# Transposed h of tiles 5 to 7 and half of one x by DMA instead of TensorE pieces, four context loads issued later, in a gated two-layer block

## The reference

```python
q1 = fake_quant(layernorm(x), x1_scale, x1_zp)      # (2, 1024, 2048)
q2 = fake_quant(ctx, x2_scale, x2_zp)               # (2, 2048, 2048)
x  = x + tanh(g_xattn[0]) * (q1 @ q2)
x  = x + tanh(g_ffn[0]) * einsum('bti,oi->bto', layernorm(x), U * S[None, :] @ V.T)
```

## Time and profile before

| | |
|---|---|
| median of 3 runs | 603.96 us (603.78 to 606.05) |
| profiled execution, its own time | 604.71 us |
| its span on the core | 602.9 us |
| granted TensorE clock | 1.0 |
| PE busy | 582.7 us, 97% |
| DVE, ACT, POOL busy | 381.7, 212.4, 191.4 us |
| DMA moved | 102.21 MB |

### The profile page before, as it was taken

One profiled execution on the slowest core, in us unless ns is written; L12 is line 12 of the kernel. 1 busy time (PEld: TensorE's weight loads), 2 busy tenths in 40 slices (PEclk: granted clock), 3 DMA queues, 4 the chain that ended last, 5 costly groups with the idle time before them and its releaser, 6 DMA issues.

```text
span 602.9 us, 7571 instructions
## 1 busy us (share of the span) xinstructions
PE 582.7 (97%) x2816; PEld 266.4 (44%) x2816; DVE 381.7 (63%) x703; ACT 212.4 (35%) x258; POOL 191.4 (32%) x149
## 2 busy tenths in 40 slices
PE   1899999999999999999999999999999999999998
PEld 1344444444444444445444444444444444444444
DVE  6939989995288962845375975647365665735212
ACT  5798978822041432456623310303011030301000
POOL 2899650002223419726505800220404030030000
DMA  8999985639828795998835344370906345181512
GB/s 280 387 387 387 309 240 128 116 122 196 239 55 240 186 216 189 241 304 268 241 123 150 81 84 54 66 190 12 223 35 147 116 90 172 30 163 20 138 53 104
DMA packets 143828, 102.21 MB, mean 170 GB/s; under 512 B 106672, under 2 KB 106928, under 8 KB 143792
## 3 DMA queue, kind: packets, MB, share of 16 engines
q1 hardware_dynamic: 134800, 84.43, 53.1%
q10 hardware_dynamic: 8992, 17.30, 9.2%
HBM read 58.99 MB, written 16.78 MB: 126 GB/s over the span
## 4 chain that ended last, share of the span: by engine, by line
PE 75%; DMA 11%; DVE 8%; issue 3%; SPq 2%; ACT 1%; POOL 1%; DVEq 0%; ACTq 0%
PE bank L553 23%; PE bank L584 16%; PE bank L651 8%; PE bank L650 8%; PE bank L655 8%; PE bank L589 8%; DMA v_hl<-in_ctx_dram 8%; DMA xT<-xs 4%; DVE v_hl L1246 1%; DVE xn L1174 1%; DVE xs L1177 1%; DVE ring L1137 1%; SPq L311 1%; PE bank L520 1%; POOL u8r L243 1%
## 5 line engine op out<-in xcount | busy, mean ns | idle before, releaser
L553 PE MATMUL bank<-q,qT 128*128 128x512 bf16 x896 | 201.5, 380 | 0.3 <-DVE ring L1137 0.3
L553 PEld LDWEIGHTS bank<-q,qT 128*128 128x128 bf16 x896 | 87.7, 98 | 107.1 <-issue 1.5
L258 POOL TENSOR_SCALAR ring<-ring,bvec 128x2048 f32<-128x2048 f32 x16 | 32.8, 2050 | 269.7 <-DVE bvec L1119 269.7
L584 PE MATMUL bank<-v_hl,xT 128*128 128x512 f16 x512 | 115.8, 379 | 0.9 <-DMA xT<-xs 0.9
L263 POOL TENSOR_TENSOR ring<-ring,corr 128x512 f32<-128x512 f32 x64 | 87.0, 1390 | 23.2 <-ACT corr L850 22.1
L651 PE MATMUL bank<-u_hl,hbuf 128*128 128x512 f16 x240 | 91.1, 380 | 0.0
L650 PE MATMUL bank<-u_hl,hbuf 128*128 128x512 f16 x240 | 91.0, 379 | 0.0
L1137 DVE SCALAR_TENSOR_TENSOR ring<-bank,const,ring 128x512 f32<-128x512 f32 x64 | 47.6, 743 | 58.2 <-PE bank L553 55.9
L1210 DVE SCALAR_TENSOR_TENSOR ring<-bank,cy,ring 128x512 f32<-128x512 f32 x63 | 46.4, 747 | 52.8 <-PE bank L655 52.8
L252 POOL TENSOR_SCALAR q<-u8r,const 128x1024 bf16<-128x1024 uint8 x52 | 63.9, 1236 | 45.4 <-ACT u8r L756 41.7
L584 PEld LDWEIGHTS bank<-v_hl,xT 128*128 128x128 f16 x512 | 49.8, 98 | 61.2 <-DMA xT<-xs 1.9
(11 more groups left out here) (136 smaller groups left out, 493.3 us busy)
## 6 DMA issues: line engine op xcount, KB each, us to landing
out_dram<-ring SPq DMA_DIRECT2D x63, 256.0 KB, 3.5
ring<-in_x_dram SPq DMA_DIRECT2D x62, 256.0 KB, 3.9
v_hl<-in_ctx_dram SPq DMA_DIRECT2D x26, 512.0 KB, 11.5
stage<-in_ctx_dram ACTq DMA_DIRECT2D x17, 512.0 KB, 5.8
u_hl<-in_L_ffn_V_dram SPq DMA_DIRECT2D x8, 512.0 KB, 11.5
corr<-in_ctx_dram ACTq DMA_DIRECT2D x8, 512.0 KB, 6.7
stage<-in_ctx_dram SPq DMA_DIRECT2D x6, 512.0 KB, 11.5
q<-in_ctx_dram ACTq DMA_DIRECT2D x4, 512.0 KB, 8.8
```

The lines of the kernel that those rows point to most:

```text
L553: mm = nc.tensor.matmul(unit_bank(t, n)[:, :], qT_of(t)[:, k, :], q2[:, n, k, :], start=(k == 0), stop=(k == KT - 1))
L584: nc.tensor.matmul(h_bank(u)[:, :], xT[:, g, half, k % 8, :], v_hl[:, k, 0, :], start=(g == 0 and a == 0 and half == 0), stop=False)
```

## The change

Transposed h of tiles 5, 6 and 7 comes by DMA from SP, and so does half g = 0 of tile 7's x. Half g = 1 stays on PE. h of tile 5 is put into `qT`'s half 1 and h of tile 7 into half 0, so two waits are new: the DMA for h of tiles 5 and 7 waits until `s1` of tile 6 or 7 is over, and `q_transpose` of tiles 8 and 9 waits until `mm4` of tile 5 or 7 has read that half. h of tile 6 stays in `hT`, and its DMA waits for `mm4(4)`. ACT issues the four `room` loads behind `x_hi_half(7, 0)` and `stream(14, 17)` instead of before `root2(7)`. The three `hT_copy` of ACT and two of the four `xT_copy` of DVE go.

```diff
+        h_home = {5: qT[:, 1, 0:2 * RT, :].bitcast(f16), 7: qT[:, 0, 0:2 * RT, :].bitcast(f16),
+                  NT - 1: qT[:, 1, 0:2 * RT, :].bitcast(f16)}
+        hT_of = lambda u: h_home.get(u, hT)
...
+                if t in (TB, TB + 1):
+                    sp.wait_ge(y_done, NQ * (6 if t == TB else 8))
                 sp.dma_start_transpose(qT_of(t), qn[:, :]).then_inc(qT_in, 16)
...
+                if u in h_home:
+                    sp.wait_ge(s1_done, S1_END({5: 6, 7: 7, NT - 1: NT - 2}[u]))
                 elif u >= 1:
-                    sp.wait_ge(y_done, NQ * u)
+                    sp.wait_ge(y_done, NQ * {6: 5, 8: 7}.get(u, u))
...
             q_transpose(7)
+            h_transpose(5)
             x_transpose(6)
             for n in range(NQ):
                 store(4, n)
             for n in range(NQ):
                 load_x(8, n)
+            x_transpose_half(7, 0)
+            h_transpose(6)
             turn(5, False)
             q_transpose(8)
+            h_transpose(7)
             turn(6, False)
...
             mm4(4)
-            h_pieces(5)
-            x_pieces(0)
             mm3(6)
-            x_pieces(1)
+            x_pieces()
             mm4(5)
-            h_pieces(6)
             mm3(7)
             mm4(6)
-            h_pieces(7)
...
             x_hi(6)
             stream(12, 14)
+            root2(7)
+            x_hi_half(7, 0)
+            stream(14, 17)
             act.wait_ge(s1_done, S1_END(TB - 1))
             for i in range(4):
                 refill(CB + ORDER.index(f"room{i}"))
-            root2(7)
-            x_hi_half(7, 0)
-            stream(14, 17)
-            hT_copy(5)
             x_hi_half(7, 1)
             stream(17, 22)
             hid_hi(6)
             stream(22, 26)
-            hT_copy(6)
...
             hid_hi(7)
             stream(30, 32)
-            hT_copy(7)
...
             x_lo_half(7, 1)
-            xT_copy(0)
             hid_lo(6)
-            xT_copy(1)
+            xT_copy()
```

More of the change, by code:

```diff
@@ L30, in gated_block_program @@
     GW = P // CG
-    H_PE = (5, 6, 7)
     X_PE = TB - 1
@@ L99, in gated_block_program @@
         qT_of = lambda t: q_in[t] if t < G else qT[:, (t + 1) % 2, :, :]
-        hT_of = lambda u: hT if u < NT - 1 else qT[:, 1, 0:2 * RT, :].bitcast(f16)
+        h_home = {5: qT[:, 1, 0:2 * RT, :].bitcast(f16), 7: qT[:, 0, 0:2 * RT, :].bitcast(f16),
+                  NT - 1: qT[:, 1, 0:2 * RT, :].bitcast(f16)}
+        hT_of = lambda u: h_home.get(u, hT)
         u_homes = [(qn[:, :].bitcast(f32), flat2(qT[:, 1, :, :]).bitcast(f32)),
@@ L124, in gated_block_program @@
         hT_in = sem("hT_in")
-        hT_written = sem("hT_written")
-        hT_copied = sem("hT_copied")
         xT_written = sem("xT_written")
@@ L195, in gated_block_program @@
         h_bank = lambda u: bank[3 + u % 2]
-        x_dma = lambda u: u + 1 - (u > X_PE)
-        x_bank = lambda g, half: bank[(2 * g + half) % 3]
-        h_dma = lambda u: u + 1 - sum(v <= u for v in H_PE)
+        x_dma = lambda u, g: u + 1 - (g == 1 and u > X_PE)
+        x_bank = lambda half: bank[half]
         ident_h = ident_b[:, :].bitcast(f16)
@@ L350, in h_transpose @@
                     sp.wait_ge(sq_done, 16)
-                if u == NT - 1:
-                    sp.wait_ge(s1_done, S1_END(NT - 2))
+                if u in h_home:
+                    sp.wait_ge(s1_done, S1_END({5: 6, 7: 7, NT - 1: NT - 2}[u]))
                 elif u >= 1:
-                    sp.wait_ge(y_done, NQ * u)
+                    sp.wait_ge(y_done, NQ * {6: 5, 8: 7}.get(u, u))
                 sp.dma_start_transpose(hT_of(u), hs.rearrange("p k w -> p (k w)")).then_inc(hT_in, 16)
@@ L570, in mm3 @@
                     pe.wait_ge(h_lo, u - 1)
-                if u - 2 in H_PE:
-                    pe.wait_ge(hT_copied, H_PE.index(u - 2) + 1)
                 if u == TB:
@@ L575, in mm3 @@
                 for g in range(2):
-                    if u == X_PE:
-                        pe.wait_ge(xT_copied, 2 * g + 2)
+                    if u == X_PE and g == 1:
+                        pe.wait_ge(xT_copied, 2)
                     else:
-                        pe.wait_ge(xT_in[g], 16 * x_dma(u))
+                        pe.wait_ge(xT_in[g], 16 * x_dma(u, g))
                     for a, k in enumerate(KORD[g]):
@@ L591, in mm3, with x_pieces @@
                     mm.then_inc(mm3_half, 1)
-            def x_pieces(g):
+            def x_pieces():
+                g = 1
+                pe.wait_ge(ident_ready, 2)
                 pe.wait_ge(xs_hi, 2 * X_PE + g + 1)
@@ L596, in x_pieces @@
                 for half in range(2):
[L597 to L601, removed]
+                    pe.wait_ge(x1_ready, S1_END(TB - 1))
+                    dst = x_bank(half)[:, :].bitcast(f16)
                     for k in range(8):
@@ L604, in x_pieces @@
                     mm.then_inc(xT_written, 1)
[L606 to L614, removed]
             def mm4(u):
[L617 to L620, removed]
+                pe.wait_ge(hT_in, 16 * (u + 1))
                 for n in range(NQ):
@@ L806, in x_hi_half @@
                 act.wait_ge(ln2_ready, u + 1)
-                if u - 1 == X_PE:
-                    act.wait_ge(xT_written, 2 * g + 2)
+                if u - 1 == X_PE and g == 1:
+                    act.wait_ge(xT_written, 2)
                 elif u > 0:
-                    act.wait_ge(xT_in[g], 16 * x_dma(u - 1))
+                    act.wait_ge(xT_in[g], 16 * x_dma(u - 1, g))
                 nc.scalar.activation(xs[:, g, 0, :], xhalf(u, g), ACT.Identity, bias=bias, scale=scale).then_inc(xs_hi, 1)
@@ L818, in hid_hi @@
                 act.wait_ge(mm3_half, 2 * u + 2)
[L819 to L822, removed]
+                if u > 0:
+                    act.wait_ge(hT_in, 16 * u)
                 else:
@@ L826, in hid_hi @@
                     .then_inc(h_hi, 1)
[L828 to L832, removed]
             def column_parts(n):
@@ L1181, in x_lo, with xT_copy @@
                 x_lo_half(u, 1)
-            def xT_copy(g):
+            def xT_copy():
                 for half in range(2):
[L1185 to L1188, removed]
+                    dve.wait_ge(xT_written, half + 1)
+                    dve.wait_ge(mm3_half, 2 * X_PE)
+                    nc.vector.tensor_copy(xT[:, 1, half, :, :].rearrange("p k w -> p (k w)"),
+                                          x_bank(half)[:, :].bitcast(f16)).then_inc(xT_copied, 1)
             def hid_lo(u):
```

## The result

The changed kernel takes 612.39 us (median of four runs, 609.71 to 613.36) against 603.97 before: ratio 1.0125, 95% interval 1.0111 to 1.014. It is 8.4 us slower by the medians and 7.5 by the ratio, which goes by all runs of both kernels; 2.9 us faster was forecast.

The account below looks back on a forecast made before the run. The kernel was taken as bound by the sum of what PE issues. Pieces spared, 2.22 us, plus the wait for x of tile 6, 0.67, made 2.89: 603.96 - 2.9 = 601.1 us, range 600.5 to 604.0.

Parts of the forecast that it names:

- What PE is spared: On PE, 40 transposes of h and x pieces at about 0.056 us each go away: 2.22 us gained.
- rival 4: On PE, each transpose piece costs the skill page's 275 ns, 11.0 us for 40, giving 592.3 us; chance 0.03.
- The wait for x of tile 6: At the second half of `mm3(6)`, PE's 0.67 us wait goes, as moving four rooms cuts the landing from 16.9 to 10.4 us.
- I take the h transpose off the path: On SP, h of tile 5 ahead of x of tile 6 costs nothing, at most 1.4 us within the spare 4.6.
- The 4.6 us to spare: At `mm3(6)`, x of tile 6 lands at 262.4, 4.6 us before PE wants it at 266.98.
- x of tile 7, half 0, issued at 267.1 and landed at 281.6: For `mm3(7)`, it takes 14.5 us and lands 1.8 us before PE wants it at 283.4: no wait.
- my bound of 272.4: On SP, the latest issue expected for the transpose of x of tile 7, half 0; the earliest was 267.1.
- the bound of 16.9: Longest landing time expected for x of tile 7, half 0; issued at 272.4 it would land at 289.3, stalling PE 5.9 us.
- The price of 1.76 us for a chunk: DMA time taken by each context chunk load, used to price landings of x of tiles 6 and 7.
- rival 1: x of tile 7 lands late for `mm3(7)`: at 284 to 286 it gives 601.7 to 603.7 us; chance 0.26.
- h of tile 6, DVE for `mm4(5)`: `hid_hi(6)` at 273.8, h landing at 283 to 285, DVE done by 276.9: no wait, bound for DVE 0.7 us.
- q of tile 9: On SP, issued after `mm4(7)` at 318.7, landing at 323.1 before L1110 at 326.0: no wait, bound 4.8 us.

Follow-up runs that it names:

- 6: Changed kernel with SP issuing h of tile 5 behind x of tile 6, and x of tile 7 ahead of tile 8's loads: 602.36 us, ratio 0.9966.
- 11: The changed kernel with both orders of SP changed, as in 6, measured again in five rounds: 601.96 us, ratio 0.9952.
- 1: Kernel before the change with only the four room loads issued later, behind chunk 17: 604.4 us, ratio 0.9995.
- 8: Changed kernel with loads of context chunks 12 to 18 of batch 1 cut to 32 of 512 columns: 609.67 us, one run.
- 7: Changed kernel with loads of context chunks 21 to 28 of batch 1 cut to 32 of 512 columns: 602.8 us, one run.
- 14: Kernel before with half 0 of tile 7's x by DMA, issued ahead of tile 8's loads, h on PE, room loads early as before: 604.04 us, ratio 1.0.
- 10: As 6, but with the room loads before root2(7) as in the kernel before the change: 609.79 us, ratio 1.0068.
- 3: Changed kernel with the room loads put back before root2(7): 618.3 us, ratio 1.022.
- 9: Changed kernel with only h of tile 5 moved behind x of tile 6 on SP: 609.2 us, ratio 1.0069.
- 2: Changed kernel with both halves of tile 7's x on PE, so only h by DMA and rooms late: 605.55 us, ratio 1.0014.
- 4: Changed kernel with the transpose of x of tile 7, half 0, ahead of tile 8's loads on SP: 606.98 us, ratio 1.0039.
- 12: Kernel before with half 0 of tile 7's x by DMA behind tile 8's loads, rooms late, h on PE: 605.19 us, ratio 1.0011.
- 13: As 12, with the transpose of x of tile 7 ahead of tile 8's loads: 603.71 us, ratio 0.9988.

## Why the prediction was wrong

*What PE is spared*: right. The pieces left at 272.18 cost 0.89 us for 16, `mm3(6)` ended where forecast, and where x is in time the gain is 2.92 us in the trace of 6 and 2.9 by the ratio of 11. The 275 ns for a transpose that the Trainium skill gives ("TensorE: Matmul & The Clock Gate", Part 4), rival 4, would have been 11.0 us, an estimate; the trace disagrees, with 0.056 us for each.

*The wait for x of tile 6*: right that the rooms made it (1: 5.3 us instead of 16.9). In the changed kernel half 1, forecast at 10.4 us and landing at 262.4, took 9.8 from 252.7.

*"I take the h transpose off the path"*: this step failed. The prediction took 3.0 to 5.8 us, from transposes with less traffic beside them, as the price of one issued at 241 us among four context chunks, though the paragraph before had priced x of tile 6 beside chunks. It took 11.7 us (8: 3.0 with those chunks thin). x of tile 6, half 0, landed 4.6 us later than before, and with it ACT, DVE, tile 4's stores and tile 8's loads were held. The 4.6 us to spare were those of half 1 and of PE; half 0, which ACT wants at 256.4 for `x_hi_half(7, 0)`, had none, and the prediction didn't price it.

*x of tile 7, half 0, issued at 267.1 and landed at 281.6*: failed by the size of both terms. It was issued at 272.59, past my bound of 272.4, and took 19.4 us, past 14.5 and past the bound of 16.9. The store that was to land in 4 us, a price for which the prediction shows no row, took 6.7; why is open, since it took 7.0 with the rooms thin (7). The price of 1.76 us for a chunk isn't general. With the chunk packets that in fact moved beside x of tile 7 it gives 15.4 us in 11 and 9.3 in 14, where 14.8 and 9.7 were measured, but 17.2 in the changed kernel (19.4) and 11.9 in 10 (20.6). In kernel 6 the forecast nearly holds, issued at 267.76 and landed at 283.0, before PE wants it.

*The clock*: no term of the sum, and none of rival 1's price. A wait of 7.6 us brought 2.8 us more at half clock. Waits of 4.3 to 5.1 us (3, 8, 9, 10) brought 1.7 to 2.9: 4.4 us brought 2.9 (10), 4.6 us 2.3 (9) and 5.1 us 1.7 (8, its first 16 matmuls in 5.14 us instead of 3.45), so the loss doesn't follow the wait's length alone. Where PE waited 2.5 us or less at a time (2, 4, 12) none was lost. With 2.8 us for the clock, rival 1's sum for a landing at 292.0 comes to 601.1 + 8.6 + 2.8 = 612.5; 612.39 was measured.

*h of tile 6, DVE for `mm4(5)`*: `hid_hi(6)` came at 278.63, not 273.8, and the bound of 0.7 us was paid, 0.83. `x_hi_half(7, 1)` ahead of it came at 269.36 instead of 264.5, behind the rooms, and these behind the late `x_hi_half(7, 0)`. h of tile 6 took 14.6 us and landed at 296.6, in time only as PE was late.

*q of tile 9*: right, no wait by it; q of tiles 8 and 9 landed in 5.6 and 4.5 us.

Rival 1, a late x of tile 7, is what happened, larger than I let it be. The rule that prefers TensorE for a 128x128 transpose (the Trainium skill, "VectorE: DVE Perf Modes", Rules for kernel authors) is borne out by the change as made, 1.0125, and not by the reordered kernel, 0.9952, which has the same pieces by DMA.

Open: what sets the time of a DMA transpose beside other traffic, and of the last store of tile 4. Chunks beside the transpose are needed (7, 8), and h transposes near it double it in one case (14 against 10), but bytes or packets beside it don't give the time.

## What to carry to other kernels

Price a transfer by rows with the same traffic beside it: the same h transpose took 3.0 us beside thin chunk loads and 11.7 beside full ones. For each transfer put ahead of another on one queue, ask who else wants the later one, besides the engine that bounds the kernel. When a change that should save time loses it, try the order on the queue before the pieces: two lines moved turned 1.25% slower into 0.3 to 0.5% faster.

## What was not expected of the hardware

A transpose of 0.52 MB took between 4.2 us and 20.8 us (kernel 3) to land. SP was held by the issue alone for 9.25 us at 272.59, and for 10.6 us by h of tile 6 at 279.0 in kernel 10; x of tile 6 had held it for 7.63 us. In kernel 7, with thin chunks beside it, the same transpose held it less than half as long:

```profile
272.39 4.15 SPq L346 DMA_TRANSPOSE xT<-xs  x1
```

With h by DMA, moving the four rooms away from x of tile 6 made x of tile 7 faster too, 14.8 against 20.6 us in kernels 11 and 10, though it put more chunks beside it. Without h by DMA it went the other way, 16.9 us with the rooms late (13) and 9.7 with them early (14).
